# Attention B: the near part of the mix as three products of rounded halves, with values and exponentials split by ScalarE, GpSimd and VectorE

## The reference, cut to what matters

```python
q = rope(einsum('bim,mhd->bhid', x, wq)); k = rope(einsum('bim,mhd->bhid', x, wk))
v = einsum('bim,mhd->bhid', x, wv)              # 16 heads, d = 128, 256 positions
s = einsum('bhid,bhjd->bhij', q * mult, k * mult)
s = s - 1e30 * (i < j)                          # causal mask
p = softmax(s)
r = einsum('bhid,hdm->bim', einsum('bhij,bhjd->bhid', p, v), wo)
```

## Time and profile before

| | us |
|---|---|
| median of 3 runs | 1560.28 (1559.67 to 1562.67) |
| the profiled execution, its own time | 1562.61 |
| its span in the profile | 1560.8 |
| attention B with its edges (743 to 1262) | 519.0 |
| PE busy over the span | 1455.4 (93%) |
| DVE busy | 1170.3 (75%) |
| ACT busy | 848.2 (54%) |
| POOL busy | 635.7 (41%) |

### The profile page before, as it was taken

One profiled execution on the slowest core, in us unless ns is written; L12 is line 12 of the kernel. 1 busy time (PEld: TensorE's weight loads), 2 busy tenths in 40 slices (PEclk: granted clock), 3 DMA queues, 4 the chain that ended last, 5 costly groups with the idle time before them and its releaser, 6 DMA issues. The chain is left out here.

```text
span 1560.8 us, 26380 instructions
## 1 busy us (share of the span) xinstructions
PE 1455.4 (93%) x8888; PEld 1262.3 (81%) x8888; DVE 1170.3 (75%) x2629; ACT 848.2 (54%) x2068; POOL 635.7 (41%) x517
## 2 busy tenths in 40 slices
PE   6599999999699999996999999999999979999998
PEld 4477777777588888885799999999999868888887
DVE  6689988899775555567888888888888777555554
ACT  3678887888333332333766666666666523333332
POOL 2578887887200000004666666666666410000000
PEclk9799999999799999997999999999999989999999
DMA  2055444445300010001332222232231200001001
GB/s 99 16 125 125 116 112 100 112 116 122 127 21 21 21 41 0 1 1 41 89 72 58 69 60 70 62 68 68 44 87 41 61 21 21 21 24 38 0 1 55
DMA packets 47542, 91.52 MB, mean 59 GB/s; under 512 B 5184, under 2 KB 25664, under 8 KB 47424
## 3 DMA queue, kind: packets, MB, share of 16 engines
q1 hardware_dynamic: 47424, 90.01, 22.9%
HBM read 29.18 MB, written 2.10 MB: 20 GB/s over the span
## 5 line engine op out<-in xcount | busy, mean ns | idle before, releaser
L1827 DVE TENSOR_TENSOR f_hidden<-ps,f_silu 128x512 f32<-128x512 f32 x128 | 87.7, 690 | 201.6 <-PE ps L116 201.5
L470 POOL TENSOR_TENSOR ab_swapped<-ab_swapped,const 128x512 f32<-128x512 f32 x124 | 160.3, 1292 | 167.8 <-ACT ab_swapped L465 167.0
L1718 ACT ACTIVATE f_silu<-ps 128x512 f32<-128x512 f32 x128 | 76.3, 598 | 277.2 <-PE ps L116 277.2
L114 PE MATMUL ps<-xh,f_wl 128*128 128x512 f32 x512 | 203.2, 397 | 1.6 <-DVE f_hidden L1827 1.6
L115 PE MATMUL ps<-xl,f_wh 128*128 128x512 f32 x512 | 202.8, 396 | 0.0
L116 PE MATMUL ps<-xh,f_wh 128*128 128x512 f32 x512 | 202.5, 396 | 0.0
L1529 POOL TENSOR_TENSOR ab_qk<-ab_qk,ab_swapped 128x512 f32<-128x512 f32 x124 | 170.0, 1371 | 9.7
L73 POOL TENSOR_TENSOR rstd<-shifted,minus_half 128x4 f32<-128x4 f32 x16 | 16.2, 1013 | 350.4 <-DVE shifted L67 347.3
L1292 ACT ACTIVATE ab_probs<-ab_probs,ab_negmax 128x128 f32<-128x128 f32 (+1 forms) x256 | 114.6, 448 | 80.1 <-DVE ab_negmax L1393 78.1
L114 PE MATMUL ps<-f_wh,f_hl 128*128 128x256 f32 x512 | 144.2, 282 | 0.4 <-DVE x L1843 0.4
L115 PE MATMUL ps<-f_wl,f_hh 128*128 128x256 f32 x512 | 143.9, 281 | 0.0
(11 more groups left out here) (208 smaller groups left out, 4428.8 us busy)
## 6 DMA issues: line engine op xcount, KB each, us to landing
ab_probsT<-ab_squares SPq DMA_DIRECT2D x128, 192.0 KB, 3.7
aa_probsT<-f_stages SPq DMA_DIRECT2D x64, 256.0 KB, 4.5
b_stages<-keys SPq DMA_DIRECT2D x64, 256.0 KB, 4.7
f_stages<-wf_in SPq DMA_DIRECT2D x16, 768.0 KB, 4.4
b_stages<-wb_qkv_in SPq DMA_DIRECT2D x8, 768.0 KB, 5.9
a_stage<-wa_in SPq DMA_DIRECT2D x8, 608.0 KB, 6.0
x<-x_in SPq DMA_DIRECT2D x4, 512.0 KB, 6.9
b_stages<-wb_out_in SPq DMA_DIRECT2D x8, 256.0 KB, 3.8
```

What stands on the lines that cost most here:

```text
L114: nc.tensor.matmul(out, ll, rh, start=start, stop=False)
L470: return engine.tensor_tensor(by_batch(out), by_batch(src), table(c, rows, col), ALU.mult)
L1827: nc.vector.tensor_tensor(hidden[:, m, :], UP(m), silu[:, m, :], ALU.mult).then_inc(hid_done, 1)
```

## The change

The values of the near keys are split in two when they leave their bank: ScalarE writes the rounded upper half `vh` (and copies the far values as before, in a second instruction), and VectorE subtracts it from the bank for the lower half `vl`. The exponentials that have landed in `probsT` are split for kinds 0 and 1: ScalarE writes `ph` (`probs_hi`, 512 columns for two pairs), GpSimd subtracts for `pl` (`probs_lo`). The near product of a mix becomes `matmul3` over these halves. The far product stays plain f32. The halves of the exponentials have one buffer for each head, so `probs_hi` waits until the mixes of the pass before have read it. TensorE waits for `p_lo` in place of the transfer, and the values bank comes free with `values_lo`. The norm's reciprocals on GpSimd are put between the last of its new work. In the opening two semaphores become one.

```diff
-        values = sb("values", [P, 2, TG, 2 * P])
+        values = sb("values", [P, 2, BG, 2 * P])
+        vh, vl = sb("vh", [P, 2, BG, 2 * P], F32R), sb("vl", [P, 2, BG, 2 * P], F32R)
+        ph, pl = sb("ph", [P, 4, 2, PAIRS, SQ], F32R), sb("pl", [P, 4, 2, PAIRS, SQ], F32R)
...
                 if j == 0:
-                    pe.wait_ge(landed[s % 2], LANDED * (2 * it + s // 2 + 1))
                     pe.wait_ge(values_done, 2 * n + 2)
                 if b == 0:
+                    pe.wait_ge(p_lo, 2 * n + h + 1)
                     after(pe, mix_lo, 2 * n + h - 1)
...
-                nc.tensor.matmul(out, v(0), columns(slice(0, 2)), start=True, stop=False)
-                nc.tensor.matmul(out[:, P:T], v(1), columns(slice(2, 3)), start=False, stop=True).then_inc(pv_done, 1)
+                column = slice(h * P, (h + 1) * P)
+                near = lambda p: p[:, :, :, j, :].rearrange("p a k i -> p k a i")
+                far = probsT[:, s % 2, :, 2, j, :]
+                matmul3(nc, out, (vh[:, s % 2, b, column], vl[:, s % 2, b, column]), (near(ph), near(pl)), True, False)
+                nc.tensor.matmul(out[:, P:T], values[:, s % 2, b, column], far, start=False, stop=True).then_inc(pv_done, 1)
...
-                nc.scalar.copy(values[:, s % 2, 2 * i:2 * i + 2, :], VALUES.rearrange("p (t d) -> p t d", t=2)).then_inc(values_done, 1)
+                nc.scalar.copy(vh[:, s % 2, i, :], VALUES[:, 0:2 * P])
+                nc.scalar.copy(values[:, s % 2, i, :], VALUES[:, 2 * P:]).then_inc(v_hi, 1)
+
+            def probs_hi(it, s, h):
+                n = slot_no(it, s)
+                act.wait_ge(landed[s % 2], LANDED * (2 * it + s // 2 + 1))
+                after(act, pv_done, PAIRS * (n - 1) + 2 * h + 2)
+                pairs = slice(2 * h, 2 * h + 2)
+                nc.scalar.copy(ph[:, :, :, pairs]..., probsT[:, s % 2, :, 0:2, pairs]...).then_inc(p_hi, 1)
...
+                if j == 1:
+                    probs_hi(it, s, 1)
+                if j == 3 and not (last and s == NG - 1):
+                    probs_hi(*moved(it, s, 0, PAIRS)[:2], 0)
...
+            probs_hi(0, 0, 0)
             head_pair(0, 0)
...
+            def values_lo(it, s, i):
+                dve.wait_ge(v_hi, 2 * slot_no(it, s) + i + 1)
+                nc.vector.tensor_tensor(vl[:, s % 2, i, :], VALUES[:, 0:2 * P], vh[:, s % 2, i, :].bitcast(F32), ALU.subtract).then_inc(values_done, 1)
...
                     row_max(*moved(it, s, j, LEAD))
+                if j == 0 and not (first and s == 0):
+                    values_lo(it, s, 1)
+                if j == 2 and not (last and s == NG - 1):
+                    values_lo(*moved(it, s, 0, PAIRS)[:2], 0)
...
                     nc.gpsimd.tensor_tensor(rows, rows, other, ALU.add).then_inc(rotated, 1)
+                    if n >= 2 and i % 2 == 1:
+                        probs_lo(n - 2, i // 2)
+
+            def probs_lo(n, h):
+                pool.wait_ge(p_hi, 2 * n + h + 1)
+                after(pool, rotated, ...)
+                nc.gpsimd.tensor_tensor(flat_pairs(pl[:, :, :, pairs]), flat_pairs(probsT[:, n % 2, :, 0:2, pairs]), flat_pairs(ph[:, :, :, pairs]).bitcast(F32), ALU.subtract).then_inc(p_lo, 1)
+                pool.wait_ge(p_lo, 2 * n + h + 1)
```

More of the change, by code:

```diff
@@ L231, in split_small @@
                 act.wait_ge(small_read, 16)
-                act.wait_ge(wr_zero, 1)
+                act.wait_ge(constants_set, 2)
                 nc.scalar.copy(c.sh[:], small_in[:, :, 0:S_WR])
@@ L326, in first_lo @@
                 nc.vector.tensor_tensor(a.ql[:, 0, h, :], a.raw[:, h, :], a.qh[:, 0, h, :].bitcast(F32), ALU.subtract).then_inc(a.q_lo, 1)
-            nc.vector.memset(c.minus_half[:], -0.5).then_inc(half_set, 1)
-            nc.vector.memset(c.wr[:].bitcast(F32), 0.0).then_inc(wr_zero, 1)
+            nc.vector.memset(c.minus_half[:], -0.5).then_inc(constants_set, 1)
+            nc.vector.memset(c.wr[:].bitcast(F32), 0.0).then_inc(constants_set, 1)
             stats(0)
@@ L378, in first_rotate @@
                 pool.wait_ge(a.rotated, h + 1)
-            pool.wait_ge(half_set, 1)
+            pool.wait_ge(constants_set, 1)
             norm_rstd(nc, c, norm, pool, 0)
@@ L1068, in attention_b @@
         rope_read, rotated, values_done = sem("rope_read"), sem("rotated"), sem("values_done")
+        v_hi, p_hi, p_lo = sem("v_hi"), sem("p_hi"), sem("p_lo")
         scores_ready, maxed, exp_done, inv_done = sem("scores_ready"), sem("maxed"), sem("exp_done"), sem("inv_done")
@@ L1299, in take_values @@
                 after(act, pv_done, PAIRS * (n - 1))
-                nc.scalar.copy(values[:, s % 2, 2 * i:2 * i + 2, :], VALUES.rearrange("p (t d) -> p t d", t=2)).then_inc(values_done, 1)
+                nc.scalar.copy(vh[:, s % 2, i, :], VALUES[:, 0:2 * P])
[5 more added lines that the diff above has]
+                pairs = slice(2 * h, 2 * h + 2)
+                nc.scalar.copy(ph[:, :, :, pairs].rearrange("p a k j i -> p a k (j i)"), probsT[:, s % 2, :, 0:2, pairs].rearrange("p a k j i -> p a k (j i)")).then_inc(p_hi, 1)
             def mixed_hi(it, s, h):
@@ L1482, in _ @@
             row_max(0, 0, 3)
+            values_lo(0, 0, 0)
             norm_lo(nc, c, own_norm, dve, 3, own_banks)
@@ L1493, in _ @@
                 turn_squares(0, 1, j)
+            values_lo(0, 0, 1)
             row_max(0, 1, 2)
@@ L1529, in rotate @@
                     nc.gpsimd.tensor_tensor(rows, rows, other, ALU.add).then_inc(rotated, 1)
+                    if n >= 2 and i % 2 == 1:
+                        probs_lo(n - 2, i // 2)
+            def probs_lo(n, h):
+                pool.wait_ge(p_hi, 2 * n + h + 1)
+                after(pool, rotated, 4 * min(n + 2, NG * HP - 1) + (2 * h + 2 if n + 2 < NG * HP else 4))
+                pairs = slice(2 * h, 2 * h + 2)
+                flat_pairs = lambda p: p.rearrange("p a k j i -> p a k (j i)")
+                nc.gpsimd.tensor_tensor(flat_pairs(pl[:, :, :, pairs]), flat_pairs(probsT[:, n % 2, :, 0:2, pairs]), flat_pairs(ph[:, :, :, pairs]).bitcast(F32), ALU.subtract).then_inc(p_lo, 1)
+                pool.wait_ge(p_lo, 2 * n + h + 1)
             for n in range(1, NG * HP):
                 rotate(n)
-            for s in range(NG):
+            for n in range(NG * HP - 2, NG * HP):
+                for h in range(2):
+                    probs_lo(n, h)
+                if n == NG * HP - 2:
+                    norm_rstd(nc, c, norm, pool, 0)
+                    pool.wait_ge(norm.rstd_done, 1)
+            for s in range(1, NG):
                 norm_rstd(nc, c, norm, pool, s)
@@ L1563, in experts @@
         gated, silu_done, hid_done, hi_done, lo_done = sem("gated"), sem("silu_done"), sem("hid_done"), sem("hi_done"), sem("lo_done")
-        out_ready, out_added, stored = sem("out_ready"), sem("out_added"), sem("stored")
+        out_ready, out_added = sem("out_ready"), sem("out_added")
         GATE = lambda m: c.ps[:, 2 * m, :]
```

4 lines of the change are left out of this document (1 added, 3 removed).

## The result

The changed kernel takes 1564.68 us (median of 8 runs, 1563.80 to 1567.41) against 1560.22 us (8 runs, 1559.67 to 1562.67) for the kernel before. The ratio is 1.0026, 95% interval 1.0016 to 1.0037: slower. The median lies above the 3.1 us (0.2%) that the prediction took as told from no change, but the interval reaches down to 0.16%. The prediction said 1562.8 us, in a range of 1554 to 1568.5, and gave 0.37 to the same and 0.35 to slower. Its own profiled execution took 1564.81 us, span 1563.0.

The account below looks back on a forecast made before the run. TensorE was taken to set the pace in steady head pairs, with VectorE arriving together with it at places. Steady part -0.8, start +2.5, end +0.8 make +2.5 on the median 1560.28: 1562.8 us, range 1554 to 1568.5.

Parts of the forecast that it names:

- VectorE takes up TensorE's saving: Steady head pairs: waits for VectorE's add_out and mixed_lo absorb TensorE's gain; likeliest case, chance 0.52, 1559.5 to 1566.5 us.
- The near product saves 0.08 us a mix: TensorE's mixes: three rounded products at 0.355 us replace one plain; 128 mixes, 10.2 us, 1.28 a head pair.
- 32-column runs: Moving side of the near product: rival that this pattern slows rounded products to 0.65 us, 1592 in all; chance 0.05.
- Given back in a head pair, 1.18 us: Output weight loads waiting for VectorE in a steady head pair: 0.50 + 0.48 + 0.20 of 1.28 us lost.
- GpSimd has 0.2 us of room at one mix: Second head's mix in the first slot: rival that GpSimd comes late there, 1568.4 us in all; chance 0.13.
- the new subtraction's risk: GpSimd's subtraction for `pl`: meeting a VectorE split could make it 0.9 us longer, 0.7 showing eight times.
- The start, +2.5: Prologue and first mixes: cast, subtraction and wake-ups delay the first mix 2.0 us, later mixes up to 1.3 more.
- The end, +0.8: Last pass, mix near 1243.73: 1.6 us late behind cast and subtraction, about half showing; between 0 and 1.6.
- the start's upper bound of 3.9 us: Prologue and first mixes together: cost put between 1.5 and 3.9 us, 2.5 taken.
- the forecast of 66.0 us for a head pair: Steady part of attention B: a head pair takes 66.0 us instead of 66.1, saving 0.10, eight save 0.8.

Follow-up runs that it names:

- rope_ahead: both_ahead with VectorE's first rope product of step 0 also moved ahead, right behind add_out; 1556.86 us, ratio 0.9974 to the kernel before.
- before_ahead: A control: the kernel before the change, with add_out and mixed_lo right behind the row maximum in VectorE's steps 0 and 1; 1559.93 us, ratio 0.9993.
- no_lower_first: Changed kernel without the product with `pl` for the first head of the first slot, TensorE waiting there for `ph` alone; 1564.54 us, ratio 1.0025.
- both_ahead: Changed kernel with add_out and mixed_lo moved right behind the row maximum in VectorE's steps 0 and 1; 1559.65 us, ratio 0.9996 to the kernel before.
- no_lower_slot0: Changed kernel without GpSimd's two subtractions and the four products that read them in the first slot; 1563.98 us, ratio 1.0022.
- plain_first_slot: Changed kernel with a plain near product in the first slot, without ScalarE's casts of `ph` and GpSimd's subtractions there; 1565.20 us, ratio 1.0027.

## Why the prediction was right, and where it was off

**VectorE takes up TensorE's saving**, the likeliest case: right. The head pair was forecast at 66.0 and is 66.03 in the mean of seven, 66.14 where it has its split. The two versions that bracket it show the mechanism: with VectorE's order changed the same products give 65.05, and with the old product in the changed kernel the head pair is only 66.44.

**The near product saves 0.08 us a mix**: too much. Free of waits the saving is 1.02 us for 16 mixes, 0.064 each, 8.2 us in all instead of 10.2. The products themselves cost what was predicted (0.12 apart, so the 32-column runs slow nothing). From the first score product to the first product behind the mix it is 1.225 us in before and 1.152 in rope_ahead, means of over a hundred steps: 0.073 saved. The rest is lost outside the group, most of it in the steps 3, and is not taken apart. The Trainium skill ("FP8 and Floating Point Precision", TensorE Precision Notes) gives true FP32 four passes through the array. If a rounded product were one of them, which the page does not say in so many words, three for four would save 0.107 us by my estimate; the runs give 60% of that.

**Given back in a head pair, 1.18 us**: measured 66.14 - 65.05 = 1.09 in a full one. The four steps 2 give 0.09 each (0.12 taken), two more steps 0 about 0.06 each (0.1 taken), and the step behind the split 5.36 - 4.75 = 0.61, for which I took 0.50. So 1.09 is given back of 1.02 saved, where I had 1.18 of 1.28. The 0.61 is 0.34 for `values_lo` (0.35 taken), 0.13 for the saving of two mixes (0.16 taken), and 0.14 because the split itself got longer, 2.22 us for 2.08, to which I gave nothing.

That last part is GpSimd's. Beside the split GpSimd multiplies by the sines, and starts ahead of it:

```profile
890.40 1.30 POOL L470 TENSOR_TENSOR ab_swapped<-ab_swapped,const 128x512 f32<-128x512 f32 x1
```

before, and in the changed kernel

```profile
891.22 1.30 POOL L470 TENSOR_TENSOR ab_swapped<-ab_swapped,const 128x512 f32<-128x512 f32 x1
```

The multiplication ends at 891.70 and the split of the earlier trace rows at 892.79; in the changed kernel they end at 892.52 and 893.60. In all six head pairs with such a split, in all fourteen kernels, the split ends 1.08 or 1.09 us behind the end of the multiplication, whether it started 0.3 us behind its start (before) or 0.03 (rope_ahead). So the end of the split is set by GpSimd, and VectorE's list alone does not set the chain to `add_out`. I also read one thing wrong in the earlier trace rows: the row maximum there starts behind the rope product, which had waited for a projection, and not as soon as the scores are there.

**GpSimd has 0.2 us of room at one mix**: right place. The changed kernel shows no such wait. When TensorE comes earlier there, it waits up to 0.8 us (both_ahead). The addition behind the split is long in every kernel (2.15 us for 1.29 alone) and ends 1.15 to 1.17 us behind the split. The Trainium skill ("SBUF — State Buffer", SBUF: two separate sides) has the two engines exclude each other for an instruction's length; these rows agree, in both directions: the split ends a fixed time behind the multiplication, and the addition a fixed time behind the split. I had put the new subtraction's risk into such a meeting. It was the queue ahead of it.

**The start, +2.5**: measured +2.42, or 1.96 against before_ahead, but by another road, so that the size came out by luck. The first mix is late as predicted (44.55 us behind the first mark for 42.65, so 1.9; 2.0 was worked out), yet taking that wait away gains nothing (no_lower_first, no_lower_slot0). What was shown: 1.2 us go with ScalarE's casts and GpSimd's subtractions of the first slot when both are gone, none with GpSimd's part alone, 0.7 us stand at a wait for `pl` in the second slot, and 0.5 us are in the control too. That ScalarE's casts alone would do it was not run. ScalarE is on this path: in the changed kernel its copies for the third slot start at 749.78, 43.97 us behind the first mark, where they started at 42.90. Its cast stands waiting for the landing ahead of them:

```profile
748.25 0.62 ACT L1313 CAST ab_ph<-ab_probsT 128x512 fp32r<-128x512 f32 x1 [0.76 <-DMA ab_probsT<-ab_squares]
...
748.95 1.27 POOL L1566 TENSOR_TENSOR ab_pl<-ab_probsT,ab_ph 128x512 fp32r<-128x512 f32 x1 [2.47 <-ACT ab_ph L1313]
...
750.36 0.36 PE L114 MATMUL ps<-ab_ph,ab_vl 128*128 128x256 f32 x1 [0.81 <-POOL ab_pl L1566]
```

**The end, +0.8**: this step failed in size, just above the upper bound of its 0 to 1.6. Measured +1.65. I took the mix near 1243.73 as 1.6 us late and let half of it hide in the wait for the adds. It is 2.9 us late: 17.58 us behind the third mark for 14.67. Most of that comes from ahead of it. The score product behind the mark waits 1.19 us for GpSimd's last rotation (0.71 before), the mix behind it 0.48 for `pl`, and at the next score product 1.22 us of the 1.65 are lost already (8.35 us behind the mark for 7.13). I had looked at one mix; the changed kernel waits for `pl` at three of the end, and the adds move with TensorE instead of covering it:

```profile
1234.78 0.38 PE L114 MATMUL ps<-ab_ph,ab_vl 128*128 128x256 f32 x1 [0.48 <-POOL ab_pl L1566]
1241.92 0.39 PE L114 MATMUL ps<-b_woh,ab_ml 128*128 128x256 f32 x1 [2.21 <-DVE x L1439]
1247.55 0.39 PE L114 MATMUL ps<-ab_ph,ab_vl 128*128 128x256 f32 x1 [1.36 <-POOL ab_pl L1566]
1253.34 0.38 PE L114 MATMUL ps<-b_woh,ab_ml 128*128 128x256 f32 x1 [1.50 <-DVE x L1439]
1257.84 0.39 PE L114 MATMUL ps<-ab_ph,ab_vl 128*128 128x256 f32 x1 [0.78 <-POOL ab_pl L1566]
```

Sum of the terms as measured: -0.22 (seven head pairs; the eighth lies in the start and the end) + 2.42 + 1.65 = +3.85, where -0.8 + 2.5 + 0.8 = +2.5 was forecast. That is 1.35 of the 1.9 us between 1562.8 and 1564.68. The other 0.5 to 0.6 is not explained; the medians moved by 4.46 and the runs of one kernel spread over 3 us.

Two smaller things in the working: the start's upper bound of 3.9 us is above what its parts give (2.0 + 1.3), and the forecast of 66.0 us for a head pair has the wrong sign for a full one.

## What to carry to other kernels

When a change makes the bounding engine faster, look for the instructions that already arrive together with it; the gain ends there, and a helper's new 0.3 us in such a chain costs its full length. Move what the bounding engine waits for (here the adds, the lower half of the mix and the first rope product) ahead of what has slack (reciprocal, transpose), all of it at once: one link alone moved the wait to the next. An instruction that ends a fixed time behind one of another engine is bounded by that engine, even where its own queue has no gap. Taking out the last wait on a path proves little while a second chain of nearly the same length stands beside it.

## What the runs showed of the hardware

TensorE's clock changes equal work near the end by more than the steady part moved. Right behind its 1.6 to 1.9 us wait for `add_out`, TensorE does the same products up to its next wait. In the execution of before the granted clock there was 0.72 on average:

```profile
1258.00:1264.00 6.00, 5.55 (x32) 5.37 (x33) 4.50 (x11) 1.66 (x3) 0.57 (x1) 0.72 0.00 0
```

in that of after it was full:

```profile
1261.00:1266.00 5.00, 4.96 (x38) 4.59 (x39) 4.53 (x11) 1.66 (x3) 0.19 (x1) 1.00 0.01 2
```

From that wait to the next the first took 1269.85 - 1258.45 = 11.40 us and the second 1271.34 - 1261.01 = 10.33. The products stood 0.21 us apart in the first (1.2 GHz) and 0.12 in the second (2.4 GHz). rope_ahead had the slow one (1251.43 to 1262.93), both_ahead the quick one (1255.75 to 1266.10), with the same work. This is why the marks end at that wait. The start has such a stretch too, behind the 2.1 us wait: before_ahead, which has it, has a start 0.46 us longer than before, which has not. The stages ahead of the change, with the same code, also brought the first mark anywhere from 704.05 to 707.10 us. One profiled execution of each kernel thus cannot be compared as a whole to better than some 2 us; between marks it can to a few tenths, if no such stretch falls between them: one of 3.4 us in the end of plain_first_slot cost 1.5 us.

VectorE's subtraction of 1024 columns with both operands in SBUF ended 1.08 us behind the end of GpSimd's multiplication beside it, in 84 of 84 cases. Of the 2.07 to 2.34 us that it lasts in the profile, 0.99 to 1.26 pass before the multiplication has ended.
